# Two-layer graph attention on one core: order of the first loads and rows, statistics and projections around the late batches, and a bank of its own for the last tile's sum

## The reference, cut to what matters

```python
h = maximum(layernorm(x), 0)
Wh = h @ W                                # 1024 x 128
e = leaky_relu(Wh @ a1 [:, None] + Wh @ a2 [None, :])
att = softmax(where(adj > 0, e, -big))    # 1024 x 1024
x = x + elu(att @ Wh)                     # layer 0
x = x + att @ Wh                          # layer 1: no elu
```

## Time and profile before

| | us |
|---|---|
| runs, median of 3 | 313.43 (313.27 to 316.34) |
| profiled execution | 314.74 |
| its span | 312.9 |
| TensorE busy | 293.6 |
| VectorE busy | 267.3 |
| ScalarE busy | 164.5 |

### The profile page before, as it was taken

One profiled execution on the slowest core, in us unless ns is written; L12 is line 12 of the kernel. 1 busy time (PEld: TensorE's weight loads), 2 busy tenths in 40 slices (PEclk: granted clock), 3 DMA queues, 4 the chain that ended last, 5 costly groups with the idle time before them and its releaser, 6 DMA issues.

```text
span 312.9 us, 6581 instructions
## 1 busy us (share of the span) xinstructions
PE 293.6 (94%) x2560; PEld 288.6 (92%) x2560; DVE 267.3 (85%) x610; ACT 164.5 (53%) x485; POOL 47.6 (15%) x53
## 2 busy tenths in 40 slices
PE   7999779799899999999999999999999999789695
PEld 7899679799899999999999999999999999788595
DVE  4596389949999989999899989999899959919785
ACT  3284480784493747483583648382674654353200
POOL 2612001220303030303003030303002000400000
PEclk9999999999999999999999999999999999999999
DMA  7997495102574334904574345713491302001211
GB/s 248 410 405 317 154 389 197 67 2 68 190 244 175 138 134 151 384 7 142 195 310 162 138 135 189 284 68 115 161 356 47 138 0 70 0 0 40 96 69 67
DMA packets 15247, 50.56 MB, mean 162 GB/s; under 512 B 2040, under 2 KB 3056, under 8 KB 15216
## 3 DMA queue, kind: packets, MB, share of 16 engines
q1 hardware_dynamic: 14640, 49.75, 43.0%
q10 hardware_dynamic: 576, 0.39, 0.4%
HBM read 45.88 MB, written 4.26 MB: 160 GB/s over the span
## 4 chain that ended last, share of the span: by engine, by line
PE 74%; DVE 10%; DMA 4%; ACT 4%; issue 4%; POOL 2%; POOLq 0%; DVEq 0%; ACTq 0%
PE acc L790 55%; PE prj L750 7%; PE tp L693 4%; DVE pbuf L564 4%; DMA row_r<-r_rows 3%; PE acc L806 2%; PE acc L690 2%; ACT xn L349 2%; POOL rstd L254 2%; DMA r_rows<-rT 1%; DVE stats L476 1%; DVE x_sb L594 1%; DVE ex L588 1%; PE prj L753 1%; DVE accs L573 1%
## 5 line engine op out<-in xcount | busy, mean ns | idle before, releaser
L790 PE MATMUL acc<-wh,pbuf 128*128 128x129 f32 x1984 | 232.9, 276 | 10.1 <-DVE accs L573 8.1
L790 PEld LDWEIGHTS acc<-wh,pbuf 128*128 128x128 f32 x1984 | 227.0, 192 | 13.3 <-issue 9.9
L564 DVE SCALAR_TENSOR_TENSOR pbuf<-row_r,sqr,adj_sb 128x1024 f32<-128x1024 f32 x127 | 157.8, 1278 | 8.8 <-DMA row_r<-r_rows 8.8
L254 POOL TENSOR_TENSOR rstd<-vareps,neg_half 128x8 f32<-128x8 f32 x15 | 37.5, 2503 | 213.9 <-DVE vareps L494 213.8
L379 ACT ACTIVATE accs<-accs,rec 128x128 f32<-128x128 f32 x120 | 36.7, 390 | 59.3 <-DVE rec L583 59.3
L349 ACT ACTIVATE xn<-x_sb,shift,rstd 128x128 f32<-128x128 f32 x120 | 47.6, 480 | 0.0
L368 ACT ACTIVATE wh<-prj,wh 128x128 f32<-128x128 f32 x120 | 31.6, 350 | 0.0
L750 PE MATMUL prj<-w_ext,hT 128*128 128x130 f32 x240 | 29.4, 275 | 0.1
L750 PEld LDWEIGHTS prj<-w_ext,hT 128*128 128x128 f32 x240 | 28.0, 191 | 0.2 <-ACT hT L355 0.2
L573 DVE TENSOR_TENSOR accs<-acc,uniform 128x387 f32<-128x387 f32 (+1 forms) x48 | 22.0, 508 | 4.2 <-PE acc L790 2.0
L476 DVE BATCH_NORM_STATS2 stats<-x_sb 128x6 f32<-128x128 f32 x120 | 24.6, 279 | 0.0
(11 more groups left out here) (81 smaller groups left out, 146.1 us busy)
## 6 DMA issues: line engine op xcount, KB each, us to landing
adj_sb<-in_adj SPq DMA_DIRECT2D x64, 512.0 KB, 6.5
row_r<-r_rows SPq DMA_DIRECT2D x15, 512.0 KB, 3.9
x_sb<-in_x SPq DMA_DIRECT2D x7, 512.0 KB, 7.1
out_x<-x_sb SPq DMA_DIRECT2D x7, 512.0 KB, 3.0
out_x<-x_sb SPq DMA_DIRECT2D x2, 192.0 KB, 1.9
x_sb<-in_x ACTq DMA_DIRECT2D x1, 256.0 KB, 3.6
x_sb<-in_x SPq DMA_DIRECT2D x1, 256.0 KB, 3.4
r_rows<-rT SPq DMA_DIRECT2D x15, 4.0 KB
```

The source lines that it names most:

```text
L254: nc.gpsimd.tensor_tensor(rstd[:, :], vareps[:, :], neg_half[:, :], ALU.pow).then_inc(rstd_ready, 1)
L564: nc.vector.scalar_tensor_tensor(pbuf[:, t, :], row_r[:, n % 2, :], sqr[:, n % 2, 0, t:t + 1], adj_at(b, t), ALU.max, ALU.min).then_inc(p_ ...
L790: mm = nc.tensor.matmul(acc[:, k, s * C:(s + 1) * C], pbuf[:, t, i * P:(i + 1) * P], wh[:, n % 2, t, :], start=(t == 0 and s == 0), stop=( ...
```

## The change

- SyncE: both halves of the first x tile are on its queue, the weights of both layers on ScalarE's, with a semaphore per layer. Row 1 is put behind five tiles of batch 1 instead of eight, row 2 behind five tiles of batch 2, and x of batches 3, 4 and 5 behind row 2 and around row 3.
- The small product of weights and attention vector (WA) is made and copied per layer; layer 1's stands behind the first projection. The warm-up counts change.
- Stage n + 1 in LATE (n = 2 and 14): projection, spread and turn_r come one attend tile sooner on TensorE, copy_hT ahead of scale_accs on ScalarE, and statistics(n + 2) behind exp_args(n + 1) on VectorE. In a LATE stage itself statistics(n + 2) stand behind exp_args(n + 1) too.
- Stage n + 2 in LATE (n = 1 and 13): turn_r comes one tile later on TensorE; on VectorE one mask (n = 1) or three (n = 13) stand ahead of the drain, and the statistics of the late stage ahead of masks 7 (n = 1) or 6 and 7 (n = 13).
- The sum of the last tile of the last stage has a bank of its own, prj's first, which ScalarE fills with the uniform part at its end (`seed_last`); VectorE finishes in four parts instead of three, the last one straight from PSUM, and SyncE stores four.

The diff, cut to its core:

```diff
-    WARM = (24, 6, 4, 3)
+    WARM = (20, 2, 2, 3)
+    last_parts = [(0, NB), (NB, 2 * NB), (2 * NB, T - 1), (T - 1, T)]
+        WA = (prj[:, 0, 0:2], acc[:, 1, 0:2])
+        LAST_TILE = prj[:, 0, 0:C]
+        def before_drain(n):
+            return 1 if n == 1 else 3 if n + 2 in LATE else 2
...
 sync:
-            sp.dma_start(w_tr[:, 0, :], w0t).then_inc(w_in, 16)
-            sp.dma_start(a_cols[:, 0, :], a0).then_inc(w_in, 16)
-            sp.dma_start(w_ext[:, 0, 0:D], w0).then_inc(w_in, 16)
+            sp.dma_start(x_sb[:, half:2 * half], xv[0][:, half:2 * half]).then_inc(x_in[0], 16)
...
-            for m in range(1, AHEAD):
-                for t in range(T):
-                    load_adj(m, t)
-                load_x(m + 2)
-                load_row(m)
-                sp.wait_ge(row_in, 16 * m)
-            load_x(AHEAD + 2)
-            load_row(AHEAD)
+            for t in range(5):
+                load_adj(1, t)
+            load_row(1)
+            sp.wait_ge(row_in, 16)
+            for t in range(5, T):
+                load_adj(1, t)
+            for t in range(5):
+                load_adj(2, t)
+            load_row(2)
+            sp.wait_ge(row_in, 32)
+            for t in range(5, T):
+                load_adj(2, t)
+            load_x(3)
+            load_x(4)
+            load_row(3)
+            load_x(5)
...
 scalar:
+            def seed_last():
+                act.wait_ge(wh_ready, T * LAST + T)
+                act.wait_ge(e_copied, 3 * LAST + 3)
+                nc.scalar.activation(LAST_TILE, uniform[:, LAST % 2, :],
+                                     ACT.Copy).then_inc(seeded_last, 1)
+            for l, (w, wt, a) in enumerate(((w0, w0t, a0), (w1, w1t, a1))):
+                nc.scalar.dma_start(w_tr[:, l, :], wt).then_inc(w_in[l], 16)
+                nc.scalar.dma_start(a_cols[:, l, :], a).then_inc(w_in[l], 16)
+                nc.scalar.dma_start(w_ext[:, l, 0:D], w).then_inc(w_in[l], 16)
...
                 elu = n > 0 and stages[n - 1][0] == 0
+                if n + 1 in LATE:
+                    copy_hT(n + 1)
                 if n > 0:
                     scale_accs(n - 1)
                 if n + 1 in LATE:
-                    copy_hT(n + 1)
                     elu_exp(n - 1) if elu else None
                     normalise(n + 2) if n + 2 <= LAST else None
                     exps(n + 1)
...
+            seed_last()
 vector, n in 1 .. LAST - 1:
-                if n + 2 <= LAST and n + 2 not in LATE and n + 1 not in LATE:
+                if n + 2 <= LAST and not {n, n + 1, n + 2} & set(LATE):
                     statistics(n + 2)
                     moments(n + 2)
-                masks(n, (0, 1))
+                masks(n, range(before_drain(n)))
                 take_acc(n - 1)
                 if n + 1 in LATE:
                     masks(n, (2, 3))
+                    copy_e(n + 1)
+                    masks(n, (4,))
+                    exp_args(n + 1)
                     if n + 2 <= LAST:
                         statistics(n + 2)
                         moments(n + 2)
-                    copy_e(n + 1)
-                    masks(n, (4,))
+                    masks(n, (5,))
+                elif n + 2 in LATE:
+                    if n == 1:
+                        masks(n, (1,))
+                        copy_e(n + 1)
+                        masks(n, (2,))
+                    else:
+                        masks(n, (3,))
+                        copy_e(n + 1)
+                        masks(n, (4,))
                     exp_args(n + 1)
-                    masks(n, (5,))
+                    masks(n, (3, 4) if n == 1 else (5,))
+                    add_elu(b)
+                    add_x(b)
+                    if n == 1:
+                        masks(n, (5, 6))
+                    statistics(n + 2)
+                    moments(n + 2)
+                    masks(n, (7,) if n == 1 else (6, 7))
+                    continue
                 else:
                     copy_e(n + 1)
                     masks(n, (2,))
                     exp_args(n + 1)
-                    masks(n, (3,))
...
+                    if n in LATE:
                         statistics(n + 2)
                         moments(n + 2)
-                        masks(n, (7,))
-                        continue
-                    masks(n, (4, 5))
+                    masks(n, (3, 4, 5))
 tensor:
+                        if t == 0 and n == LAST and i == T - 1:
+                            pe.wait_ge(seeded_last, 1)
...
                 if n + 1 in LATE:
                     attend(n, (0,))
                     transposes(n + 1)
-                    attend(n, (1, 2))
+                    attend(n, (1,))
                     project(n + 1)
+                    attend(n, (2,))
+                    spread_emax(n + 1)
                     attend(n, (3,))
-                    spread_emax(n + 1)
-                    attend(n, (4,))
                     turn_r(n + 1)
-                    attend(n, (5,))
+                    attend(n, (4, 5))
                 else:
                     project(n + 1)
                     attend(n, (0,))
                     spread_emax(n + 1)
-                    attend(n, (1,))
+                    attend(n, (1, 2) if n + 2 in LATE else (1,))
                     turn_r(n + 1)
-                    attend(n, (2, 3, 4, 5))
+                    attend(n, (3, 4, 5) if n + 2 in LATE else (2, 3, 4, 5))
```

More of the change, by code:

```diff
@@ L109, in gat_two_layers @@
         const_set = sem("const_set")
-        wa_done = sem("wa_done")
-        wext_ready = sem("wext_ready")
+        wa_done = [sem(f"wa_done{l}") for l in range(2)]
+        wext_ready = [sem(f"wext_ready{l}") for l in range(2)]
         bn_half = sem("bn_half")
@@ L443, in means_first, with copy_wa @@
                                         ALU.mult).then_inc(mean0_ready, 1)
+            def copy_wa(l):
+                dve.wait_ge(wa_done[l], 1)
+                nc.vector.tensor_copy(w_ext[:, l, D:E], WA[l]).then_inc(wext_ready[l], 1)
             def statistics_first():
@@ L461, in statistics_first @@
                 dve.wait_ge(mean0_ready, 2)
+                copy_wa(0)
                 for t in range(HALF, T):
@@ L624, in _ @@
             statistics(1)
+            copy_wa(1)
             copy_e_first()
@@ L659, in _ @@
                     exp_args(n + 1)
-                    masks(n, (3,))
-                    if n + 2 in LATE:
-                        add_elu(b)
-                        masks(n, (4,))
-                        add_x(b)
-                        masks(n, (5, 6))
+                    if n in LATE:
                         statistics(n + 2)
                         moments(n + 2)
-                        masks(n, (7,))
-                        continue
-                    masks(n, (4, 5))
+                    masks(n, (3, 4, 5))
                 if l == 0:
@@ L678, in _ @@
                     masks(n, (6, 7))
-            masks(LAST, (0, 1))
+            masks(LAST, range(before_drain(LAST)))
             take_acc(LAST - 1)
@@ L690, in keep_warm, with project_a @@
                     nc.tensor.transpose(acc[:, 0, 0:P], ident[:, :], ident[:, :])
+            def project_a(l):
+                pe.wait_ge(w_in[l], 48)
+                nc.tensor.matmul(WA[l], w_tr[:, l, :], a_cols[:, l, :], start=True, stop=True,
+                                 skip_group_check=True).then_inc(wa_done[l], 1)
             def turn(t):
@@ L772, in turn_r, with sum_of @@
                                     ident[:, :]).then_inc(r_turned, 1)
+            def sum_of(n, i):
+                k, s = bank_of[i]
+                return LAST_TILE if n == LAST and i == T - 1 else acc[:, k, s * C:(s + 1) * C]
             def attend(n, tiles):
@@ L803, in attend_last @@
                             pe.wait_ge(p_ready, T * LAST + t + 1)
[L804 to L810 removed]
+                        for i in range(lo, hi):
+                            mm = nc.tensor.matmul(sum_of(LAST, i), pbuf[:, t, i * P:(i + 1) * P],
+                                                  wh[:, LAST % 2, t, :], start=False,
+                                                  stop=(t == T - 1), skip_group_check=True)
                     mm.then_inc(acc_done, 1)
@@ L814, in _ @@
             keep_warm(WARM[0])
-            pe.wait_ge(w_in, 96)
-            for l in range(2):
-                mm = nc.tensor.matmul(prj[:, 0, 2 * l:2 * l + 2], w_tr[:, l, :], a_cols[:, l, :],
-                                      start=(l == 0), stop=True, skip_group_check=True)
-            mm.then_inc(wa_done, 1)
+            project_a(0)
             keep_warm(WARM[1])
@@ L822, in _ @@
             project_first()
+            project_a(1)
             hsum_first(range(HALF))
```

68 lines of the change are left out of this document (31 added, 37 removed).

## The result

The changed kernel is slower: 324.32 us in the median against 313.84 us of the kernel before beside it, ratio 1.029, interval 1.0236 to 1.0345. The direction and the wait before turn_r(3) were forecast, the size was not: 316.6 had been said, in a range of 311 to 319.5. The profiled execution took 324.39 us with a span of 322.6, 9.7 more than before.

The account below looks back on a forecast made before the run. TensorE, with 74% of the chain, was taken to bound the kernel, VectorE close behind. Terms -4.2 + 6.6 + 1.7 + 2.5 - 5.6 + 2.2 = +3.2 us on a 313.43 median gave 316.6, range 311 to 319.5.

Parts of the forecast that it names:

- Startup: Start to attend(0,0), at 15.36 before: shorter warm-up lets the first transposes start sooner, gain 1.0 us (0.4 to 1.3).
- Row 1: Up to mask(1,0): with fewer loads queued ahead, the first row's write is quicker, gain 2.2 us.
- The write falls to 1.2: Write of row 1 on SyncE's queue: 3.42 us before, 1.2 once the queue is empty at 25 us.
- rival D: Row 1's write stays at 3.4 us, being the first of its kind; 318.8 us, chance 0.10 together with rival C.
- Stage 1: From mask(1,0) to transposes(3): VectorE sets the pace, its wait for ScalarE's elu is gone; -1.0 us.
- rival C: Later loads delay row 2 and attend(2,0) by 1 us, startup gives only 0.4; 319 us, 0.10 with rival D.
- Stage 2 and the clock: transposes(3) to attend(3,0): TensorE waits 8.7 us before turn_r(3), +6.6 us, plus +2.5 for half clock behind it.
- Rival A: Both new waits come but TensorE's clock is kept, so the gap costs only its length; 314.1 us, chance 0.20.
- Stage 3: attend(3,0) to attend(4,0): statistics(5) ahead of mask 3 delay VectorE's masks; +1.7 us (0.9 to 2.2).
- The end: Stages 13 and 14: earlier masks and statistics(15) bring attend(15,0) sooner; -5.6 us (-4.5 to -6).
- The seed and the tail: Last stage: TensorE waits for seed_last behind scale_accs(14), +2.2 us; VectorE's four final parts change 0.
- Rival B: The wait at turn_r(3) is absent or hidden, dropping stage 2, stage 3 and clock terms; 305.8 us, chance 0.10.

Follow-up runs that it names:

- e3: Changed kernel with layer 0's weight loads on SyncE's queue behind the x halves, ahead of x of batch 1; 321.49 us, ratio 1.0159.
- f2: Kernel before with only the change's SyncE order of loads and rows; 313.72 us, ratio 0.9971.
- e1: Changed kernel with exps(3) and copy_r(3) ahead of normalise(4) on ScalarE, likewise in the other LATE stage; 318.31 us, ratio 1.0109.
- e7: Changed kernel with statistics and moments (4) back ahead of copy_e(3), and (5) ahead of masks(3,0); 313.04 us, ratio 0.9922.
- e2: Changed kernel with 72 constant transposes filling TensorE's wait between attend(2,3) and turn_r(3); median 323.1 us, ratio 1.0244.
- f3: Kernel before with only the change's orders for stages 13 and 14, without the last tile's bank; 307.82 us, ratio 0.979.
- e9: Changed kernel with the startup loads and warm-up counts of before, semaphore per layer kept; 319.2 us, ratio 1.0125.
- e10: Changed kernel with the edits of e9, e1, e7 and e4 together; 304.45 us, ratio 0.9645.
- e11: e10 plus a 4 KB dummy write to the row's device memory ahead of the tiles of batch 1; 304.03 us, ratio 0.9635.
- e4: Changed kernel with seed_last ahead of scale_accs(14) on ScalarE; 320.01 us, ratio 1.0169.
- f1: Kernel before, unchanged, profiled a second time; no run time given, the first row's write took 3.33 us.
- f4: e10 without the last tile's bank, with three parts at the end; ratio 0.9646, executions from 302.59 to 308.64 us.

## Why the prediction was right or wrong

- **Startup, forecast -1.0, measured +2.4.** The step that failed is "project_a(0) and two more end by about 6.6": it puts the wait for the weights at nothing. I asked when x lands, and that part held (VectorE takes up the second half at 5.33, as before), but never when w_ext lands once the weights stand alone on ScalarE's queue beside x of batch 1 and the adjacency. It landed 6.8 us after its issue, and project_a(0) ran at 8.46. The lower bound was not low enough either: I had priced a slow warm-up at 0.6, but the low clock behind the gap of 2.48 us cost 1.3 (9.28 against 8.00 in e3). The gain itself, from the shorter warm-up, is not shown: with it kept and the weights ahead of the bulk, e3 starts attend(0,0) at 15.28, where before had 15.36.
- **Row 1, forecast -2.2, measured -0.5.** The step "The write falls to 1.2" failed. The bandwidth argument was right about the queue (0 GB/s from 26 to 31 us in the changed kernel) and wrong about the write, which has a long value even then, and had it in the profiled execution (31.09 to 34.19, 3.10). This is what rival D said, given less than 0.10, though for another reason: the write is not always long the first time. In f2 it took 1.25, and mask(1,0) came 2.7 sooner, as the term had it.
- **Stage 1, forecast -1.0, measured -1.0.** VectorE's sum from mask(1,0) on held, and rival C's late second row did not come.
- **Stage 2 and the clock, forecast +9.1, measured +9.4.** The chain exp_args(3), statistics(4), power, normalise(4), exps(3) came out at 8.69 us of wait where 8.7 was said. The clock term was 6.43 - 3.74 = 2.7 instead of 2.5. e1 and e7 show the cause from both ends, e2 the clock's part in one execution. Rival A (the clock kept) is out.
- **Stage 3, forecast +1.7, measured +3.0.** The first wait was right, the rest in the wrong place. The wait before mask 3 was 1.17 (0.9 said). The other 0.8 I had put at the end, where VectorE would be late for attend(4,0); that came without a wait. What I had put at nothing is the wait for normalise(5) before transposes(5), 1.43: statistics(5) came later, and `shift` on GpSimd, between masks, took longer than the 0.2 to 0.9 of before.

```profile
97.08 2.61 POOL L270 TENSOR_TENSOR rstd<-vareps,neg_half 128x8 f32<-128x8 f32 x1 [22.18 <-DVE vareps L524]
99.77 2.02 POOL L273 TENSOR_TENSOR shift<-negmean,rstd 128x8 f32<-128x8 f32 x1
```

  (GpSimd's timeline of the changed kernel.) e7 gives the stage back its 17.40.
- **The end, forecast -5.6, measured -5.2.** f3 confirms it: -5.5 between attend(4,0) and attend(15,0).
- **The seed and the tail, forecast +2.2, measured +1.7.** The number is near, but not by the forecast's way alone. At full clock the seed costs 1.8 of wait and 2.0 in all (e2, e3, e9 against e10 and e11), and 0.3 is won at the tail. In the changed kernel the wait was 0.24, and the rest of the time went into tiles at low clock behind a gap of 2.18, which the forecast did not have. That the two overlapped instead of adding up is luck.

Taken together, 5.1 of the 6.5 us missed lie in the first 38 us of the kernel, behind two landings of DMAs (the weights', with the low clock that followed, and the first row's write); 1.3 more lie in stage 3. These are the parts of one execution; how the other executions divide is not known. Rival B, 305.8 for a kernel without the stage 2 wait, was not what the change does, but it is near what e10 measured, 304.45. That nearness is partly chance: e10 has neither the seed's wait nor the startup gain that B counted.

## What to carry to other kernels

When a block is moved on one engine, look at every other engine whose fixed order has something behind that block's result: here statistics moved on VectorE, and ScalarE still had normalise ahead of exps, so the row of the next stage waited for statistics it does not need. Small loads that gate the start belong ahead of bulk loads, not beside them on another queue, where a 0.3 KB packet takes its turn with a 1.9 KB one. And a wait of TensorE must be priced twice: its length, and the slow tiles that may follow it, even where it is no longer than 2.1 us.

## What the runs showed of the hardware that was not expected

- TensorE's granted clock fell to half behind gaps of 8.69, 3.81 (e1), 3.23 (e7), 3.14 (e1), 3.12 (e4), 2.92 (f1), 2.87 (f2), 2.18 (the changed kernel) and 2.06 us (f4), and stayed up behind 2.98 (the kernel before), 2.04 (e11), 2.00 (e2), 1.99 (e9), 1.94 (e3), 1.92 (e10), 1.89 (f3) and 1.78 (e7). Between 2.06 and 2.98 the length of the gap did not decide.
- At the start it went low for about 3.4 us behind a gap of 2.1 to 3.2 us that followed a warm-up of 3.9 to 4.5 us, in the changed kernel, e1, e2, e4 and e7; behind the gap of 1.57 in e3 and none in e9 it did not. In e11 and f4 (14.5 to 17.5 us) and once more in e1 (16.4 to 19.6 us) it was low although the view of waits lists no wait of TensorE between 11 and 20 us.
- The first write of a row takes either 1.24 or over 3 us on an idle queue; in all four long ones two of the 16 packets came 1 to 1.5 us behind the others.
